# A language-model layer on one core: query side and values as three products of split operands, and moments, decays, fills and tail put elsewhere

## The reference

```python
x = emb[tokens] * sqrt(256) + pos_enc                         # [16, 256, 256]
qk = (x @ w_q) @ (x @ w_k).T / sqrt(256)
h = softmax(qk, axis=queries) @ (x @ w_v)
u = layernorm(layernorm(h)) * ln_w + ln_b
z, xBC, dt = split(u @ in_proj.T)                             # 512, 768, 8
xBC = silu(conv4(xBC) + conv_b);  dt = softplus(dt + dt_bias)
y = ssd(xs * dt, dt * A, B, C) + D * xs                       # chunks of 128 tokens, 8 heads of 64
y = rmsnorm(y * silu(z)) * norm_w
h = h + (y @ out_proj.T + layernorm(h))
w, e = top2(softmax(layernorm(h) @ w_router))                 # 8 experts, 1024 places each
h = h + scatter_add(w * (gelu(xb @ w1[e]) @ w2[e])) + bias    # xb: rows of each expert, FF 1024
```

## Time and profile before

| what | value |
|---|---|
| median of 3 runs | 941.9 us (941.37 to 942.46) |
| the profiled execution | 941.01 us |
| its span, first to last instruction | 939.3 us |
| mean granted TensorE clock | 0.994 |
| TensorE busy | 909.7 us, 97% |
| VectorE busy | 639.8 us, 68% |
| ScalarE busy | 530.3 us, 56% |
| GpSimd busy | 495.7 us, 53% |

### The profile page before, as it was taken

How to read it: one execution, slowest core, us unless ns; L and a number is a source line. 1 busy time by engine, 2 the same in 40 slices (tenths; PEclk the granted TensorE clock), 3 DMA queues, 4 the chain that set the end, 5 groups by cost and what they waited for, 6 DMA issues and landing times.

```text
span 939.3 us, 17898 instructions
## 1 busy us (share of the span) xinstructions
PE 909.7 (97%) x5898; PEld 813.8 (87%) x5898; DVE 639.8 (68%) x1691; ACT 530.3 (56%) x1097; POOL 495.7 (53%) x496
## 2 busy tenths in 40 slices
PE   7999999999999999999999889999999999999997
PEld 6988888888888888888888779999999999999986
DVE  2487899889988898889889544646464646464642
ACT  1666776677667766776677233535344544444432
POOL 5447876887678767876685521223232323233343
PEclk9999999999999999999999999999999999999999
DMA  7930011001000100010000125253535253433221
GB/s 221 318 98 12 35 46 34 22 34 33 13 22 13 24 13 22 14 25 12 13 14 4 36 94 147 43 134 58 124 60 123 62 117 67 112 72 63 23 57 46
DMA packets 48503, 58.22 MB, mean 62 GB/s; under 512 B 6304, under 2 KB 43787, under 8 KB 48464
## 3 DMA queue, kind: packets, MB, share of 16 engines
q1 hardware_dynamic: 35024, 41.23, 13.7%
q0 software_dynamic: 13440, 16.50, 10.7%
HBM read 33.62 MB, written 29.75 MB: 67 GB/s over the span
## 4 chain that ended last, share of the span: by engine, by line
PE 82%; DVE 9%; DMA 3%; issue 2%; POOL 1%; ACT 1%; DVEq 0%; POOLq 0%; another core or an unknown queue 0%; ACTq 0%; SPq 0%
PE bank L1770 12%; PE bank L1768 12%; PE bank L1769 12%; PE bank L1507 12%; PE bank L1619 6%; PE bank L1452 4%; PE bank L1600 3%; PE bank L1491 3%; PE bank L1473 3%; PE bank L1482 3%; PE bank L1466 3%; PE bank L1572 2%; DVE seg L1141 2%; PE bank L1439 2%; DMA out<-ye,tok_slot 2%
## 5 line engine op out<-in xcount | busy, mean ns | idle before, releaser
L682 POOL DMA_INDIRECT out<-ye,tok_slot x56 | 97.4, 1740 | 248.6 <-DMA out<-ye,tok_slot 119.6
L953 ACT ACTIVATE hf<-bank 128x512 f32<-128x512 f32 x128 | 79.3, 620 | 185.1 <-PE bank L1770 184.9
L1387 DVE TENSOR_TENSOR h_lo<-hf,h_hi 128x512 fp32r<-128x512 f32 x128 | 88.6, 692 | 102.9 <-ACT h_hi L955 102.8
L1768 PE MATMUL bank<-w_hi,h_hi 128*128 128x256 f32 x512 | 146.1, 285 | 0.0
L1769 PE MATMUL bank<-w_lo,h_hi 128*128 128x256 f32 x512 | 144.9, 283 | 0.0
L1770 PE MATMUL bank<-w_hi,h_lo 128*128 128x256 f32 x512 | 144.8, 283 | 0.0
L1104 DVE SCALAR_TENSOR_TENSOR xc<-bank,cw,xc 128x253 f32<-128x253 f32 (+2 forms) x288 | 128.2, 469 | 1.5
L1768 PE MATMUL bank<-xe_hi,w_hi 128*128 128x512 f32 x256 | 99.9, 390 | 0.2 <-DVE xe_lo L1379 0.2
L1770 PE MATMUL bank<-xe_hi,w_lo 128*128 128x512 f32 x256 | 99.8, 390 | 0.1
L1769 PE MATMUL bank<-xe_lo,w_hi 128*128 128x512 f32 x256 | 99.8, 390 | 0.0
L615 POOL DMA_INDIRECT slots_dram<-rows,slot x64 | 63.5, 993 | 67.4 <-DVE slot L1248 52.6
(11 more groups left out here) (214 smaller groups left out, 2354.0 us busy)
## 6 DMA issues: line engine op xcount, KB each, us to landing
w_raw<-w SPq DMA_DIRECT2D x16, 1024.0 KB
slots_dram<-zero_row SPq DMA_DIRECT2D x1, 8320.0 KB, 30.6
xe<-slots_dram SPq DMA_DIRECT2D x15, 520.0 KB, 4.5
out<-hb SPq DMA_DIRECT2D x16, 256.0 KB, 2.1
w_raw<-in_wT SPq DMA_DIRECT2D x2, 644.0 KB, 6.3
slots_dram<-rows,slot POOLq DMA_INDIRECT x64
out<-ye,tok_slot POOLq DMA_INDIRECT x64, 3.8
xe<-slots_dram SPq DMA_DIRECT2D x2, 260.0 KB, 3.1
```

The lines of the kernel that those rows point to most:

```text
L682: g.indirect_dma_start(out, bass.IndirectOffsetOnAxis(ap=tok_slot[q][:, j:j + 1], axis=0), ye[q][:, j, :], None, compute_op=ALU.add).then_ ...
L953: sc.activation(hf[m % 2][:, :], h_bank[i % H_BANKS][:, :], ACT.Gelu_apprx_tanh)\
L1387: vc.tensor_tensor(h_lo[:, m, :], hf[m % 2][:, :], h_hi[:, m, :].bitcast(F32), ALU.subtract)\
L1768: te.matmul(out_, hi, rhi, start=first_, stop=False)
```

## The change

In every half with a back, `query_side` and `values` become three products of split operands. The low and high parts of `xT` are made by VectorE (`embedded_low`) and ScalarE (`embedded_high`) a half ahead; those of `wqk` and `wv` once, in the first half. The moments `lm`, `lv` leave the end of a half and go behind the next half's score maximum. `decay_scores` of the second chunk goes ahead of `router_top`, and its `own_chunk` ahead of `choices_before`. Both low halves of `w_in` are made on GpSimd. The fillers' numbers change, the drain's order too. Spare rows of the output (1024 where 128 were) take an expert's places that no token fills, each its own row. The last writes wait for their landing once, at the end, and no longer each for itself.

```diff
-        FILL = dict(t=4, scores=4, attend=7, hT=30, dt=12)
-        DRAIN = dict(rows=2, seg0=2, rows1=8, state=6, yT1=5, out=4)
-        LAST = dict(v2T=19, route=2, choices=8)
+        FILL = dict(t=4, scores=4, attend=5, hT=18, dt=8)
+        DRAIN = dict(rows=2, seg0=1, seg2=8, state=2, out=2)
+        LAST = dict(v2T=10, route=2, choices=9)
...
+            sp.dma_start(out[T:T + CAP, :].rearrange("(j p) n -> p j n", p=P),
+                         zero_row[:, 0:DM].unsqueeze(1).to_broadcast([P, JS, DM])).then_inc(s_dump, 16)
...
-            pool.wait_ge(w_in_split, KD)
-            g.tensor_tensor(w_in_lo[:, 1, :], w_in[:, 1, :], w_in_hi[:, 1, :].bitcast(F32), ALU.subtract)\
-                .then_inc(w_in_split, 1)
+            def low_half(k):
+                pool.wait_ge(w_in_split, KD + k)
+                g.tensor_tensor(w_in_lo[:, k, :], w_in[:, k, :], w_in_hi[:, k, :].bitcast(F32), ALU.subtract)\
+                    .then_inc(w_in_split, 1)
+            low_half(0)
...
                         second_root(t, p)
                         gated_root(b, q)
                         with_bias(t, p)
-                        describe_rows(t, p)
                         second_root(b, q)
-                        with_bias(b, q)
-                    else:
-                        describe_rows(t, p)
+                    describe_rows(t, p)
                     scatter_rows(t, p)
-                    free_rows(t, p)
...
                 norm_roots(f, p)
+                if not b:
+                    low_half(1)
...
-                    pool.wait_ge(added, 16 * (JS * (NE - 1) + j + 1))
+                pool.wait_ge(added, 16 * JS * NE)
...
+            def embedded_high(r, p):
+                act.wait_ge(xT_ready[p], xT_ready.now(r, p))
+                copy(flat(xT_hi[p][:, :, :]), flat(xT[p][:, :, :]), xT_high[p])
...
+                    copy(flat(wqk_hi[:, :, :]), flat(wqk[:, :, :]), s_high)
+                    copy(flat(wv_hi[:, :, :]), flat(wv[:, :, :]), s_high)
...
+            def embedded_low(r, p):
+                dve.wait_ge(xT_high[p], xT_high.now(r, p))
+                vc.tensor_tensor(xT_lo[p][:, :, :], xT[p][:, :, :], xT_hi[p][:, :, :].bitcast(F32), ALU.subtract)\
+                    .then_inc(xT_low[p], 1)
...
-            dve.wait_ge(w_in_split, 1)
-            vc.tensor_tensor(w_in_lo[:, 0, :], w_in[:, 0, :], w_in_hi[:, 0, :].bitcast(F32), ALU.subtract)\
-                .then_inc(w_in_low0, 1)
...
                 if f:
                     query_max(f, p)
+                if f and t:
+                    residual_moments(t, p)
...
                     times_dt(b, q, 1)
+                if b:
+                    decay_scores(b, q, 1)
                 if t:
                     router_top(t, p)
                 if b:
-                    decay_scores(b, q, 1)
                     first_y(b, q)
...
                     count_choices(p)
+                if nf:
+                    embedded_low(nf, q)
...
                     conv(f, p, 2)
+                if f and not b:
+                    for n, (low, whole, high) in enumerate(((wqk_lo, wqk, wqk_hi), (wv_lo, wv, wv_hi))):
+                        dve.wait_ge(s_high, n + 1)
+                        vc.tensor_tensor(low[:, :, :], whole[:, :, :], high[:, :, :].bitcast(F32), ALU.subtract)\
+                            .then_inc(s_low, 1)
                 if b and nf:
-                    residual(b, q)
+                    residual_sum(b, q, q)
+                    residual_stats(b, q)
...
+            def split_product(out_, hi, lo, rhi, rlo, first_, last_):
+                te.matmul(out_, hi, rhi, start=first_, stop=False)
+                te.matmul(out_, hi, rlo, start=False, stop=False)
+                return te.matmul(out_, lo, rhi, start=False, stop=last_)
...
                     pe.wait_ge(xT_ready[p], xT_ready.now(r, p))
+                    if b:
+                        pe.wait_ge(s_low, 2)
+                        pe.wait_ge(xT_low[p], xT_low.now(r, p))
...
+                            if b:
+                                ins = split_product(dst, wqk_hi[:, k, at], wqk_lo[:, k, at], xT_hi[p][:, k, :],
+                                                    xT_lo[p][:, k, :], k == 0, k == KD - 1)
+                            else:
+                                ins = te.matmul(dst, wqk[:, k, at], xT[p][:, k, :], start=(k == 0), stop=(k == KD - 1))
...
                     x_to_rows(b, q, 0)
+                    x_to_rows(b, q, 1, p)
...
-                    choices_before(t, p)
                     return
                 if not f:
                     keep_clock(p, LAST["v2T"])
                     to_v2T(t, p)
+                    choices_before(t, q)
                     keep_clock(p, LAST["route"])
...
+                if b:
+                    own_chunk(b, q, 1)
                 if t:
                     choices_before(t, p)
                 if b:
-                    own_chunk(b, q, 1)
                     to_yT(b, q, 0)
...
-                    for j in range(4):
-                        if j == 2:
-                            pe.wait_ge(xe_loaded[0][0], 16)
-                        for k in range(KD):
+                    for k, signal_ in ((0, first_half), (1, xeT_psum)):
+                        for j in range(4):
+                            if k == 0 and j == 2:
+                                pe.wait_ge(xe_loaded[0][0], 16)
                             ins = te.transpose(x_bank[k][:, j * P:(j + 1) * P], xe[0][:, j, k * P:(k + 1) * P],
                                                ident[:, :])
-                    ins.then_inc(xeT_psum, 1)
+                        ins.then_inc(signal_, 1)
```

More of the change, by code:

```diff
@@ L185, in lm_block @@
         wv = fb("wv", [P, KD, DM])
+        wqk_hi, wv_hi = (fb(name, [P, KD, DM], F32R) for name in ("wqk_hi", "wv_hi"))
+        wqk_lo, wv_lo = (fb(name, [P, KD, DM], F32R) for name in ("wqk_lo", "wv_lo"))
         w_in_hi = fb("w_in_hi", [P, KD, in_wT.shape[1]], F32R)
@@ L210, in lm_block @@
         xT = pair("xT", [P, KD, L])
+        xT_hi = pair("xT_hi", [P, KD, L], F32R)
+        xT_lo = pair("xT_lo", [P, KD, L], F32R)
         tT = pair("tT", [P, KD, L])
@@ L280, in lm_block @@
         tok_slot = [eb(f"tok_slot{q}", [P, JS], I32) for q in range(2)]
+        unfilled = [eb(f"unfilled{q}", [P, JS]) for q in range(2)]
         second.close()
@@ L827, in end_decay, with late_rows @@
                 copy(edec[p][:, :], seg[p][:, 0, :, P - 1], edec_ready[p])
+            def late_rows(r, p):
+                act.wait_ge(xdt_ready[p], xdt_ready.now(r, p))
+                copy(xs[p][:, 1, :], bank[1 - p][2][:, :], xs_ready[p])
             def x_rows(r, p, c):
@@ L835, in state, with square @@
                 copy(st[p][:, :], bank[p][3][:, :], st_ready[p])
+            def square(r, p, c):
+                act.wait_ge(y_ready[p], y_ready.now(r, p, c + 1))
+                ins = sc.activation(sz[p][:, c, :], y[p][:, c, :], ACT.Square, accum_out=ss[p][:, c:c + 1])
+                if c == KD - 1:
+                    ins.then_inc(ss_ready[p], 1)
             def squares(r, p):
@@ L1182, in residual_sum @@
                     for c in range(KD):
-                        ins = vc.scalar_tensor_tensor(out=h2[p][:, c, :], in0=bank[p][0][:, c * DM:(c + 1) * DM],
+                        ins = vc.scalar_tensor_tensor(out=h2[p][:, c, :], in0=bank[where][0][:, c * DM:(c + 1) * DM],
                                                       scalar=rms[p][:, c:c + 1], in1=hu[p][:, c, :],
@@ L1191, in residual_norm, with residual_moments, residual @@
                     norm_stats(own, p, h2[p], stats2[p], mv2[p])
+                    own.close()
+                def residual_moments(r, p):
+                    own = Chain(dve, residual_chain, RESIDUAL_LINKS, r, p)
+                    own.wait(RESIDUAL_LINKS)
                     vc.tensor_scalar(lm2[p][:, :], mv2[p][:, :, 0], -1.0, None, ALU.mult)
                     vc.tensor_scalar(lv2[p][:, :], mv2[p][:, :, 1], EPS, None, ALU.add).then_inc(lv2_ready[p], 1)
-                    own.close()
-                def residual(r, p):
-                    residual_sum(r, p)
-                    residual_norm(r, p)
+                def residual(r, p, where):
+                    residual_sum(r, p, where)
+                    residual_stats(r, p)
+                    residual_moments(r, p)
                 def router_in(t, p):
@@ L1311, in half @@
                     slots_of(t, p)
+                if not f:
+                    with_bias(t, p)
                 if nf:
@@ L1471, in values @@
                     for c in range(KD):
+                        dst, at = bank[p][2][:, c * DM:(c + 1) * DM], slice(c * P, (c + 1) * P)
                         for k in range(KD):
-                            ins = te.matmul(bank[p][2][:, c * DM:(c + 1) * DM], xT[p][:, k, c * P:(c + 1) * P],
-                                            wv[:, k, :], start=(k == 0), stop=(k == KD - 1))
```

(9 more changed lines are left out.)

108 lines of the change are left out of this document (69 added, 39 removed).

## The result

The changed kernel takes 948.0 us, the median of 20 runs, against 942.44 of the kernel before in 20 runs: a ratio of 1.0053, 95% interval 1.003 to 1.0076. It is half a per cent slower. The runs lie wider apart than before: from 941.08 to 955.71, where the kernel before has 940.4 to 945.28. That spread turns out to be the point of the case. The profiled execution took 948.66, with a span of 946.9.

The account below looks back on a forecast made before the run. VectorE with GpSimd was taken to bound the loop at 31.2 us a half, TensorE nearly so. Start +6.9, loop +5.9, drain -8.7, tail -2.9 on the profiled 941.0 gave 942.2, median 943.0; range 927 to 948.5.

Parts of the forecast that it names:

- the loop's term: Thirteen equal halves of the loop: +0.45 us each from products, decay order and rounding, +5.9 in all.
- Start: Second half's query side waits for `wv_lo`, held by GpSimd's segment products, moving 37.7 to 44.3; with low clock after, +6.9 us.
- Products, +0.65 a half: Loop: making `xT_lo` on VectorE, between `conv 0` and `conv 1` where it has no gap, costs 0.65 us a half.
- 5.06 loses only the short wait ahead of the maximum, some 0.1: Loop: with the second decay product moved, VectorE's 5.06 us from `lnv` to the first `y` shrinks by only 0.1.
- Moments, nothing: Loop: moments behind the score maximum gain nothing, since `seg` starts only when `seg_lo` is about to end.
- its rule on two inputs in SBUF: A VectorE instruction with two SBUF inputs and a GpSimd instruction reading SBUF exclude each other for their whole length.
- The second rival: Loop: moments come too late and GpSimd waits for `lv`; 0.5 us a half, +6.5, 949.5; chance 0.12.
- `shift` behind the earlier `seg`, "in the sum as nothing": Loop: GpSimd's `xs` delayed by nothing to 1.2 us, making `hn` wait; hidden by VectorE's longer circle, so no cost.
- Drain, -8.7: Drain: eight scatters without a gap end 7.5 us earlier, first rows come 1.2 earlier; -8.7, bounds -6 and -10.5.
- The split of the first rows: Drain: transposes, then a cast on each of two engines, take about 1.2 us off the first expert product's start.
- Tail, -2.9: After the last expert: with one wait at the end the last write starts at about 933.5, not 936.30; bounds -2.5, -3.5.

Follow-up runs that it names:

- e11: The changed kernel with the two subtractions for the lows of `wqk` and `wv` right behind `dt_in` of the first half; 934.65 us, ratio 0.9918.
- e1: The changed kernel with the second decay product behind the router's top again and `own_chunk` of the second chunk behind `choices_before`; 947.45 us, ratio 1.007.
- e13: The kernel before with only the second decay product ahead of the router's top and its `own_chunk` ahead of `choices_before`; 940.88 us, ratio 0.9999.
- e7: The changed kernel with the two moments ahead of the score maximum again; 942.77 us, ratio 1.0007.
- e2: The changed kernel with plain fp32 products for query side and values in every half, without the split parts of `xT`, `wqk` and `wv`; 933.99 us, ratio 0.9921.
- e4: The changed kernel with plain fp32 products for query side and values in the second half alone; 936.63 us, ratio 0.9953.
- e8: The changed kernel with a wait behind each of the last eight writes again; 949.97 us.
- e9: The changed kernel with `choices_before` of the batch before the last back at the end of the first drain half; 951.66 us, ratio 1.0113.
- e3: The changed kernel with five filler matmuls between `own_chunk` of the first chunk and `to_hT` in halves with routing; 944.42 us, ratio 1.0036.
- e5: As e4, with the two subtractions moved ahead of the second half's score maximum and two fillers ahead of `to_hT`; 934.41 us, ratio 0.9915.
- e10: The changed kernel with three filler matmuls ahead of `own_chunk` of the first chunk, none ahead of `to_hT`; 942.21 us, ratio 1.0002.
- e12: As e11, with the plain second-half products of e4 and two fillers ahead of `to_hT`; 931.95 us, ratio 0.9898.

## Why the prediction came out as it did

The measured 948.0 lies inside the range (927 to 948.5), near its upper end. The number named was 943.0, and the chances were 0.40 for faster, 0.35 for slower and 0.25 for the same; the kernel is 0.5% slower. That it stays in the range is in part luck: the loop's term was 5 us too high, and that hides most of the 6.8 of the falls, which stood in no term. With the loop as forecast, the same falls would give 953. By the prediction's own steps:

**Start: right, and its mechanism shown.** Query side was to move from 37.7 to 44.3 and did to 44.94; the subtractions waited for GpSimd's segment products at the seams, as forecast, and the low clock followed (0.50 to 49 us). e11 shows the cause by taking it away: 0.69 each, and 11.6 us less.

**Products, +0.65 a half: right in kind, 0.5 in size.** `xT` to `msq` grew by 0.51 (7.08 to 7.59), and e1, which has the products without the moved decay, runs at 31.71, 0.5 over before.

**"5.06 loses only the short wait ahead of the maximum, some 0.1": mis-sized.** The stretch fell from 5.06 to 4.68. The order with and without the move differs by 31.71 - 31.28 = 0.43 a half beside the products, and by 0.18 in e13. This is the larger part of what failed in the loop: +0.45 forecast, +0.08 measured, 5 us over thirteen halves. The rows say where the time lies, though no run isolates it. The router's small steps `topf` and `oh` stand beside GpSimd's `xs` and are held: 0.98 and 0.99 in e1, 0.68 and 0.99 before, 0.46 and 0.99 in the changed kernel; in every second half of e13, where `seg` is held for 2.00 in their place, 0.17 and 0.19. A `seg` ahead of them takes up part of the time that they would stand waiting.

**Moments, nothing: right, by the reason given.** `seg` still ends 1.1 after `seg_lo`, although it is issued 0.6 earlier in the circle (`msq` to `seg` 10.01 instead of 10.61, and `seg` 0.65 longer). e7 puts the size at 0.10. The prediction read the 1.26 of `lv` by its rule on two inputs in SBUF; `lv` reads one tile, `mv`, and is held all the same, so the rows carry the reading and that rule doesn't. The second rival, the late moments, lay closer than its 0.12: `lv` is 0.98 late in e2.

**`shift` behind the earlier `seg`, "in the sum as nothing": the step that failed.** Its size was named (nothing to 1.2) and came out at 0.9. It was true that VectorE's circle hides it. But the sum asked only what TensorE's 0.6 us of idle time cost as time, and not what they do to the clock. With the shorter products they make TensorE wait on both sides of `own_chunk`, and in some halves the clock then falls, mostly 2.2 to 2.3 us each.

The five kernels with both waits (the changed one, e4, e8, e9, e11) spread over 13.8, 8.4, 7.6, 8.9 and 4.6 us. The kernels of the change where one of them is missing, filled, or moved (e1, e2, e3, e5, e7, e10, e12) spread over 4.0, 2.7, 3.6, 1.8, 3.2, 3.1 and 2.3. The two groups nearly touch, with 4 to 20 runs a kernel. And in the old order runs scatter without the pair: e13 spreads over 7.0, and the kernel before, whose one wait is that for `seg`, over 4.9, 6.7, 8.9 and 4.1 in its four sets of runs. What is shown, then, is that every recorded fall follows the wait for `hn`, and that filling either wait makes the changed kernel's runs faster and closer. That both waits together are the condition is not shown.

The fastest of the changed kernel's runs, 941.08, is near what the other terms alone give: 939.3 + 7.6 + 1.0 - 6.1 + 0.4 - 2.1 = 940.1 of span, and 1.7 around it. The median is three falls above it.

**Drain, -8.7: mis-sized, -6.1.** `lmax` came where forecast, 28.95 after the drain's start (28.4 to 32). The last scatter ends 5.7 earlier in the drain, where 7.5 were forecast. The eight scatters were not seamless: 1.4 us lie between the fourth and fifth, in which GpSimd writes the rows' description, and the first of them waits 2.2 for slots, as `choices_before` moved. The split of the first rows brought 0.3 of its 1.2: TensorE waits 4.44 for them and then runs them at the low clock (9.0 us from the last scatter's end to the first product before, 8.7 after).

**Tail, -2.9: -2.1, mechanism shown by e8.** The last write starts 0.8 after the end of the last `ye`, not 0.1.

What stays open: why a fall comes in some halves and not in others of the same pattern, and why one of them lasted 13.6 us. The kernel before has runs up to 947.95 at a mean clock of 0.984 as well, so it isn't free of them; none of its slower runs has a profile, so where its clock falls isn't known.

## What to carry to other kernels

Price an idle time of TensorE twice: as time on the path, and as a danger to its clock. A wait of 0.6 us that another engine's circle hides was followed here, in some halves, by a fall of the clock that cost 2 us, and two fillers there cost nothing of the period (31.26) and kept the runs within 2.3 us. When two elementwise engines are both busy in SBUF, look where the other one is before placing a one-time step: the same two subtractions cost 1.4 us of VectorE's time in one place, and put the loop's start 11.6 us later in another. And read the spread of the runs with the granted clock beside it, before the median.

## What the runs showed of the hardware that was not expected

- The time of one program on one core scattered by 13.8 us (941.08 to 954.84, mean clock 0.990 to 0.978), in an otherwise regular loop. Eight of the nine recorded falls took the clock to the 1.2 GHz level for 3.4 us each, at 2.2 to 2.3 us of time (1.6 for the second one of e11); one, in e4, lasted 13.6 us and cost 6.2. All nine began 0.1 to 0.5 us after a wait of 0.58 to 0.60 had ended.
- Total activity doesn't tell whether the clock holds. From 88 to 370 us, a stretch with no fall in either profile, TensorE was busy for 273.19 us in e1, whose clock held to the loop's end, and for 274.80 in the changed kernel, whose clock fell at 376 us.
- A VectorE instruction that was issued in the middle of a GpSimd one is recorded with its waiting: `seg` 1.88 instead of 1.23, ending when it did before. By the trace alone it looks as if it had become slower. By the Trainium skill (SBUF — State Buffer, "Who interferes with whom"), a VectorE instruction with two inputs in SBUF contends with a GpSimd instruction that reads SBUF. The trace agrees: `xdec`, issued while `seg` waits, takes 2.02 (2.05 before), where the one at 49.60 us of the kernel before, issued just ahead of a `seg`, took 1.04.
